# Expert results added to the tokens' rows in DRAM by accumulating indirect transfers, in a two-layer attention and mixture-of-experts kernel

## The chip, the cores and the metric

The kernel runs on one core of a Trainium2 chip. The metric is the device time of one execution in microseconds (us), as a median of several runs. TensorE (PE) multiplies matrices, VectorE (DVE) and ScalarE (ACT) work on tiles, GpSimd (POOL) works on tiles and issues the indirect transfers, and SyncE (SP) issues plain transfers, as ACT does too. An indirect transfer moves one row for each of 128 partitions, to or from the row of a DRAM table that a tile of indices names.

## The reference

Two layers over 2048 tokens of width 256. Each layer is cross-attention onto 154 context rows, then a mixture of 8 experts, of which each token uses two.

```python
x = x + L0_xattn(layernorm(x), ctx, ...)      # 16 heads
x = x + L0_ffn(layernorm(x), ...)             # 8 experts, top 2, inner width 1024, SiLU
x = x + L1_xattn(layernorm(x), ctx, ...)      # one head, with a bias that is given
x = x + L1_ffn(layernorm(x), ...)             # 8 experts, top 2, inner width 512, GELU
# L1_ffn: an expert keeps the first cap = 640 of its tokens, others are dropped
exp_batches = zeros((E, cap, d)).at[flat_e, pos_safe].set(x[tok], mode='drop')
exp_out = einsum('eci,eid->ecd', h, W2)
gathered = exp_out[flat_e, minimum(pos_safe, cap - 1)]
contrib = where(keep, gates_f, 0.0)[:, None] * gathered
out = segment_sum(contrib, tok, num_segments=N)
```

The last four lines are what the change touches: an expert's result for a token is scaled by the token's gate weight and added to the token's row, two results for each token.

## The kernel before

The sum `x` lies in SBUF as 16 tiles of 128 tokens, in 4 groups `g` of 4 tiles. All steps are written out by hand for each engine, in one program with semaphores; what stands behind a waiting instruction on its engine waits too.

A layer's mixture begins with routing. DVE's `choose`, `place` and `count` find each token's two experts, its slot in each (`slot_s`, expert times `REGION` plus position) and the two weights. POOL's `scatter(l, g)` (L520) sends each tile's normalised rows to the table `rows` in DRAM, once for each of the two choices: 8 indirect transfers for each group, 32 in a layer. SP's `clear_padding` fills the end of each expert's region with zeros. `count` writes a table of blocks: each expert has as many blocks of 256 rows as its tokens need, and PE does the last of them at half width where half is enough (21 blocks in layer 0 and 19 in layer 1 in this run).

`experts(l)` on PE, ACT and DVE then goes through the experts' blocks. In each block PE computes gate and up products in `pairs` steps (4 in layer 0, 2 in layer 1), ACT and DVE turn them into the hidden values in two float16 parts, PE turns the next block's rows (`turn_block`), and then multiplies down into PSUM banks 4 and 5. PE is up to two steps ahead of ACT and DVE, but the down product of block g waits for `y` of block g-1, since it writes the same banks. ACT ends a block by asking for the rows of block g+2 (`load`, L1087), copying the banks to the one buffer `yb` (L1111, signal `y`) and storing it in the table `results` (L1113).

Weights come beside that. SP fetches chunks of 512 KB into a ring of three, ACT makes the high part of each (`high_part`, L974) in the first block of the expert before, and POOL the low part (`low_parts`, L511: 6 chunks an expert in layer 0, 3 in layer 1). PE waits for the low parts of an expert before its first block.

When all blocks are stored, POOL gathers the results (`gather`, L544: two indirect transfers for each tile) and DVE adds them with their weights to `x` (`combine`, L1574 and L1576). Between the layers `combine_group(0)` and the layer norm behind it come ahead of PE's first work in layer 1 (`turn("a1", 0, ...)`, L620). In `layernorm` the tiny steps from L1193 to L1203 take an inverse square root. At the end, every combined tile is stored to the output.

## Time and profile before

| | us |
|---|---|
| median of 3 runs (1058.75 to 1060.64) | 1059.73 |
| the profiled execution, its own time | 1060.89 |
| its span | 1059.1 |

| engine | busy us | share of the span |
|---|---|---|
| PE | 749.0 | 71% |
| DVE | 540.3 | 51% |
| ACT | 392.6 | 37% |
| POOL | 374.8 | 35% |

The span is the profiled execution from its first to its last instruction; the run's own time is 1.8 us longer. Shares of busy time are means over stages with different limits, so each stage is read by itself. A row of the timeline gives the start, the duration, the engine, the line, the operation, what it writes and reads, and in brackets how long the engine was idle before it and what ended that. "issue" is time in which the engine waited for nothing that the profile shows.

### The profile page before, as it was taken

What the parts mean: (1) busy time and instruction counts of PE and PEld (TensorE: products, weight loads), DVE (VectorE), ACT (ScalarE), POOL (GpSimd) and SP (SyncE); (2) the same over time, 40 slices, a digit from 0 to 9 for tenths busy, and PEclk for the clock granted to TensorE, in tenths of its full rate; (3) what the DMA queues carried; (4) which work ended last, traced back from release to release, by engine and by line L of the source; (5) the groups of instructions that cost most, each with busy time, mean ns of one, the idle gap of its engine ahead of it and who ended that gap; (6) DMA issues with size and microseconds to landing.
All of it is one profiled execution on the core that took longest, in us unless ns stands there. A gap on an engine that the chain in (4) does not pass through costs nothing.

```text
span 1059.1 us, 18158 instructions
## 1 busy us (share of the span) xinstructions
PE 749.0 (71%) x6305; PEld 574.3 (54%) x6319; DVE 540.3 (51%) x1292; ACT 392.6 (37%) x668; POOL 374.8 (35%) x281
## 2 busy tenths in 40 slices
PE   5586969775249998998799891788734777777700
PEld 4243636534138887897588780354423665666600
DVE  7776768787514443453244643478652334434322
ACT  1136555593124354454445431222202344434300
POOL 7326005073724050451543407433232125132065
PEclk9888988797669999999899995666655999999955
DMA  4557114023324141541443213311013333241243
GB/s 122 149 117 272 31 34 117 1 85 123 110 70 159 40 139 40 159 139 42 139 156 99 89 39 90 100 40 41 35 43 129 120 119 127 91 148 50 69 129 119
DMA packets 68999, 103.81 MB, mean 98 GB/s; under 512 B 12406, under 2 KB 49923, under 8 KB 68956
## 3 DMA queue, kind: packets, MB, share of 16 engines
q1 hardware_dynamic: 39964, 64.82, 19.9%
q10 hardware_dynamic: 22848, 22.03, 6.5%
q0 software_dynamic: 6144, 16.44, 4.9%
q8 instruction: 21, 0.34, 0.1%
q14 instruction: 22, 0.18, 0.1%
HBM read 69.74 MB, written 33.87 MB: 98 GB/s over the span
## 4 chain that ended last, share of the span: by engine, by line
PE 39%; issue 25%; DVE 14%; ACT 9%; POOL 9%; DMA 3%; ACTq 1%; POOLq 0%; DVEq 0%
PE ps L595 36%; POOL probs L511 3%; DVE probs L1567 2%; POOL slot L511 2%; DVE probs L1495 2%; DVE mx L1350 2%; ACT probs L1034 2%; PE ps L620 1%; POOL rows L526 1%; DMA heads<-results,slot_g 1%; POOL heads L544 1%; ACT probs L1105 1%; ACT expo L1031 1%; DVE stats L1184 1%; ACT probs L974 1%
## 5 line engine op out<-in xcount | busy, mean ns | idle before, releaser
L1562 DVE TENSOR_TENSOR keys<-probs,ps 128x512 f32<-128x512 f32 x122 | 82.8, 687 | 304.3 <-PE ps L595 235.8
L595 PE MATMUL ps<-keys,probs 128*128 128x256 f16 (+1 forms) x1584 | 150.6, 257 | 25.3 <-issue 23.0
L595 PE MATMUL ps<-keys,slot 128*128 128x256 f16 (+1 forms) x1344 | 145.8, 273 | 20.8 <-issue 17.9
L511 POOL TENSOR_TENSOR probs<-inbox,probs 128x1024 f16<-128x1024 f32 x36 | 84.9, 2375 | 199.0 <-ACT probs L974 198.9
L595 PEld LDWEIGHTS ps<-keys,probs 128*128 128x128 f16 x1584 | 132.6, 99 | 41.9 <-issue 25.2
L595 PEld LDWEIGHTS ps<-keys,slot 128*128 128x128 f16 x1344 | 124.4, 102 | 41.0 <-issue 21.7
L511 POOL TENSOR_TENSOR slot<-inbox,slot 128x1024 f16<-128x1024 f32 x36 | 82.7, 2314 | 119.5 <-ACT slot L974 119.4
L1101 ACT ACTIVATE probs<-ps 128x512 f32<-128x512 f32 x122 | 71.4, 596 | 138.3 <-PE ps L595 135.1
L1567 DVE TENSOR_TENSOR probs<-keys,probs 128x512 f16<-128x512 f32 x122 | 116.6, 960 | 4.7 <-ACT probs L1105 1.9
L544 POOL DMA_INDIRECT heads<-results,slot_g x64 | 64.5, 1008 | 123.4 <-DMA results<-keys 79.2
L595 PE MATMUL ps<-probs 128*128 128x256 f16 x648 | 75.4, 273 | 16.0 <-DVE probs L1567 16.0
L1105 ACT CAST probs<-keys 128x512 f16<-128x512 f32 x122 | 74.8, 614 | 25.8 <-DVE keys L1562 25.6
L1495 DVE TENSOR_TENSOR probs<-expo,probs 128x512 f16<-128x512 f32 x80 | 63.7, 812 | 34.2 <-ACT probs L1034 33.9
L595 PE MATMUL ps<-slot,probs 128*128 128x256 f16 x600 | 69.7, 273 | 14.7 <-DVE probs L1567 14.7
L595 PEld LDWEIGHTS ps<-probs 128*128 128x128 f16 x648 | 61.1, 98 | 26.6 <-DVE probs L1567 19.5
L595 PEld LDWEIGHTS ps<-slot,probs 128*128 128x128 f16 x600 | 56.8, 98 | 24.4 <-DVE probs L1567 18.1
L1031 ACT ACTIVATE expo<-ps 128x512 f32<-128x512 f32 x80 | 47.8, 600 | 47.5 <-PE ps L595 44.6
L1111 ACT COPY keys<-ps 128x512 f32<-128x512 f32 x40 | 23.4, 585 | 111.1 <-PE ps L595 111.1
L526 POOL DMA_INDIRECT rows<-xp,slot_s x48 | 50.5, 1051 | 32.2 <-DVE slot_s L1434 16.6
L854 PE MATMUL ps<-identh,probs 128*128 128x128 f16 x336 | 26.4, 223 | 40.8 <-DMA probs<-rows 40.8
L1034 ACT CAST probs<-expo 128x512 f16<-128x512 f32 x80 | 49.0, 618 | 0.0
L555 POOL CAST xp<-xln 128x256 f16<-128x256 f32 x16 | 7.3, 456 | 113.0 <-ACT xln L981 111.5
(236 smaller groups left out, 1140.2 us busy)
## 6 DMA issues: line engine op xcount, KB each, us to landing
inbox<-in_W SPq DMA_DIRECT2D x24, 512.0 KB, 3.8
probs<-rows ACTq DMA_DIRECT2D x44, 256.0 KB, 2.7
results<-keys ACTq DMA_DIRECT2D x40, 256.0 KB, 2.1
inbox<-in_wg SPq DMA_DIRECT2D x16, 512.0 KB, 4.6
inbox<-in_wu SPq DMA_DIRECT2D x16, 512.0 KB, 3.5
inbox<-in_wd SPq DMA_DIRECT2D x16, 512.0 KB, 3.4
results<-zeros SPq DMA_DIRECT2D x6, 1024.0 KB, 10.9
rows<-zeros SPq DMA_DIRECT2D x16, 256.0 KB, 2.0
```

The lines of the kernel that those rows point to most:

```text
L511: pool.tensor_tensor(w_hl[slot][:, 1, at:at + CH], stage[:, n % STAGES, :], w_hl[slot][:, 0, at:at + CH], ALU.subtract).then_inc(S(f"w_rea ...
L526: pool.indirect_dma_start(out=rows, out_offset=bass.IndirectOffsetOnAxis(ap=slot_s[:, g * GT + t, k:k + 1], axis=0), in_=xps[g % 2 if l.n ...
L544: pool.indirect_dma_start(out=gb[:, t % GT, k, :], out_offset=None, in_=results, in_offset=bass.IndirectOffsetOnAxis(ap=slot_g[:, t, k:k + ...
L595: return pe.matmul(o, l, r, start=start, stop=stop, **kw)
L854: last = pe.transpose(psh[:, 6, part * BLK + hf * P:part * BLK + (hf + 1) * P], x_raw[:, hf, part * P:(part + 1) * P], identh[:, :])
L1031: act.activation(e_ring[:, u % 4, :], ps[:, 4 + u % 2, :], ACT.Exp, scale=float(DK) ** -0.5).then_inc(S("a0_exp"), 1)
L1034: act.copy(p_hi[:, u - 1, :], e_ring[:, (u - 1) % 4, :]).then_inc(S("a0_phi"), 1)
L1101: act.activation(s_act[:, j % 2, :], ps[:, 2 * (j % 2), :], l.act).then_inc(S(r + "_s"), 1)
L1105: act.copy(h_hi[:, 2 * j - 2:2 * j, :].rearrange("p c t -> p (c t)"), h32[:, (j - 1) % 2, :]).then_inc(S(r + "_hh"), 1)
L1495: dve.tensor_tensor(p_lo[:, u, :], e_ring[:, u % 4, :], p_hi[:, u, :], ALU.subtract).then_inc(S("a0_plo"), 1)
L1562: dve.tensor_tensor(h32[:, j % 2, :], s_act[:, j % 2, :], ps[:, 2 * (j % 2) + 1, :], ALU.mult).then_inc(S(r + "_h32"), 1)
L1567: dve.tensor_tensor(h_lo[:, 2 * j - 2:2 * j, :].rearrange("p c t -> p (c t)"), h32[:, (j - 1) % 2, :], h_hi[:, 2 * j - 2:2 * j, :].rearran ...
```

## The change

ACT no longer copies a block's result out of PSUM; it scales each row by its weight on the way (two activations with a scale for each partition) and stores nothing. Weight and token number of each slot come from a new DRAM table `meta` (8 bytes a row), loaded for each block into the tile `carried`. POOL fills that table by 32 more indirect transfers in each layer (`scatter_weights`), and for each block it issues two indirect transfers that add `yb`'s rows to the tokens' rows in a DRAM array (`add_results`): `attended` in layer 0, the output itself in layer 1. Both start as a copy of `x`, which SP writes (`keep_rows`). Between the layers SP loads `attended` back into `x`. The table `results`, its filling with zeros, the gathers, the adding on DVE and the stores at the end are gone, and so are the index and weight steps of DVE that served them. A row past the end of an expert's tokens has the token number `FAR`, which is out of bounds, and so is skipped.

```diff
+            def keep_rows(l, g, signal):
+                sp.dma_start(l.sums[g * GW:(g + 1) * GW, :].rearrange("(t p) d -> p t d", p=P), x[:, g * GT:(g + 1) * GT, :]).then_inc(S(signal), 16)
+            def added(l):
+                total = sp.value_load(table[l.n][0:1, 8:9], min_val=1, max_val=MAXBLK)
+                wait_counted(sp, S(l.r + "_added"), total + 1)
...
-            for n in range(k0 + STAGES):
+            for n in range(STAGES):
+                fetch(L[0], 0, n)
+            for g in range(NG - 1):
+                sp.wait_ge(S("a0_x"), 2 * (g + 1))
+                keep_rows(L[0], g, "r0_kept")
+            for n in range(STAGES, k0 + STAGES):
                 fetch(L[0], n // k0, n % k0)
...
+                if e == 0:
+                    added(L[0])
+                    for g in range(NG):
+                        sp.dma_start(x[:, g * GT:(g + 1) * GT, :],
+                                     attended[g * GW:(g + 1) * GW, :].rearrange("(t p) d -> p t d", p=P)).then_inc(S(f"r0_x{g}"), 16)
...
+            def add_results(l, e):
+                tb, r = table[l.n], l.r
+                first = pool.value_load(tb[0:1, bass.ds(e, 1)], min_val=0, max_val=MAXBLK - 1)
+                end = pool.value_load(tb[0:1, bass.ds(e + 1, 1)], min_val=1, max_val=MAXBLK)
+                with pool.Fori(first, end) as g:
+                    wait_counted(pool, S(r + "_y"), g + 2)
+                    for hf in range(2):
+                        pool.indirect_dma_start(
+                            out=l.sums, out_offset=bass.IndirectOffsetOnAxis(ap=carried[:, hf, 1:2].bitcast(I32), axis=0),
+                            in_=yb[:, hf, :], in_offset=None, bounds_check=N - 1, oob_is_err=False,
+                            compute_op=ALU.add).then_inc(S(r + "_stored"), 16)
+                    pool.wait_ge(S(r + "_stored"), g * 32 + 32)
+                    pool.sem_inc(S(r + "_added"), 1)
...
             def rest_of_experts(l):
+                pool.wait_ge(S(l.r + "_kept"), 16 * NG)
+                pool.wait_ge(S(l.r + "_table"), 1)
                 low_parts(l, 1, 1, range(len(l.chunks)))
-                with pool.Fori(1, E // 2) as pr:
+                add_results(l, 0)
+                with pool.Fori(0, E // 2 - 1) as pr:
                     for slot in range(2):
-                        low_parts(l, pr * 2 + slot, slot, range(len(l.chunks)))
+                        low_parts(l, pr * 2 + slot + 2, slot, range(len(l.chunks)))
+                        add_results(l, pr * 2 + slot + 1)
+                add_results(l, E - 1)
...
+            def scatter_weights(l, g):
+                for t in range(GT):
                     for k in range(TOP):
                         pool.indirect_dma_start(
-                            out=gb[:, t % GT, k, :], out_offset=None, in_=results,
...
+                            out=l.meta, out_offset=bass.IndirectOffsetOnAxis(ap=slot_s[:, g * GT + t, k:k + 1], axis=0),
+                            in_=sent[:, g * GT + t, k, :], in_offset=None, bounds_check=E * REGION - 1,
+                            oob_is_err=False).then_inc(S(f"{r}_meta"), 16)
...
+                def load_carried(g):
+                    row = act.value_load(tb[0:1, bass.ds(g + TB_ROW, 1)], min_val=0, max_val=E * REGION - BLK)
+                    act.wait_ge(S(r + "_added"), g + 1)
+                    act.dma_start(carried[:, :, :], l.meta[bass.ds(row, BLK), :].rearrange("(h p) d -> p h d", p=P)).then_inc(S(r + "_carried"), 16)
...
                     load(g + 2)
+                    load_carried(g)
                     act.wait_ge(S(r + "_down"), g + 2)
-                    act.wait_ge(S(r + "_stored"), g * 16 + 16)
-                    act.copy(yb[:, :, :], ps[:, 4:6, 0:D]).then_inc(S(r + "_y"), 1)
-                    act.wait_ge(S(r + "_y"), g + 2)
-                    act.dma_start(results[bass.ds(g * BLK, BLK), :].rearrange("(h p) d -> p h d", p=P), yb[:, :, :]).then_inc(S(r + "_stored"), 16)
+                    act.wait_ge(S(r + "_carried"), g * 16 + 16)
+                    for hf in range(2):
+                        ins = act.activation(yb[:, hf, :], ps[:, 4 + hf, 0:D], ACT.Identity, scale=carried[:, hf, 0:1])
+                    ins.then_inc(S(r + "_y"), 1)
...
                 load(1)
+                act.wait_ge(S(r + "_meta"), 16 * NT * TOP)
                 with act.Fori(0, E // 2 - 1) as pr:
...
-            def combine(l, t):
+            def rows_summed(g):
+                dve.wait_ge(S(f"r0_x{g}"), 16)
                 layernorm("a1", g, xln, g)
```

On POOL, the order changes at three kinds of places. First the end of routing in layer 0, where `rows` is the table of the tokens' rows. Before:

```order
L557 TENSOR_TENSOR xp<-xln,xp 128x256 [waits pool_step]
L526 DMA rows<-xp,slot_s 18432x512 [waits r0_slot,r0_xp]
L526 DMA rows<-xp,slot_s 18432x512 x7
L511 TENSOR_TENSOR probs<-inbox,probs 128x1024 [waits w_hi0] x6
L516 UNCONDITIONAL_BRANCH
```

And of the changed kernel, where the lines are other numbers for the same code and `meta` is the new table:

```order
L573 DMA rows<-xp,slot_s 18432x512 [waits r0_slot,r0_xp]
L573 DMA rows<-xp,slot_s 18432x512 x7
L585 DMA meta<-sent,slot_s 18432x2 x16
L538 TENSOR_TENSOR probs<-inbox,probs 128x1024 [waits w_hi0,r0_table,r0_kept]
L538 TENSOR_TENSOR probs<-inbox,probs 128x1024 [waits w_hi0] x5
```

Sixteen transfers of groups 2 and 3 now stand behind the last rows; those of groups 0 and 1 stand behind their own groups' rows. Layer 1 has the same order. Next on POOL, the end of layer 0's experts. Before:

```order
L516 REGISTER_ALU
L516 COMPARE_AND_BRANCH
L573 TENSOR_TENSOR betas<-betas 128x1 [waits ld_phi]
L575 TENSOR_TENSOR betas<-betas 128x1 [waits pool_step]
L577 TENSOR_SCALAR keys<-keys,betas 128x2464 [waits pool_step]
L533 TENSOR_LOAD table
```

And of the changed kernel, with the last expert's loop of adding ahead:

```order
L549 DMA attended<-keys,carried 2048x256 [waits r0_y]
L549 DMA attended<-keys,carried 2048x256
L553 ISA
L546 REGISTER_ALU [waits r0_stored]
L546 COMPARE_AND_BRANCH
L618 TENSOR_TENSOR betas<-betas 128x1 [waits ld_phi]
L620 TENSOR_TENSOR betas<-betas 128x1 [waits pool_step]
L622 TENSOR_SCALAR keys<-keys,betas 128x2464 [waits pool_step]
L538 TENSOR_TENSOR slot<-inbox,slot 128x1024 [waits w_hi1] x3
```

The scaling of the attention bias (`keys` here, `phi` in the source) was free to run once the last low parts were made; now it and layer 1's first low parts stand behind the last block's adding. Last on ACT, the end of a block in layer 0. Before:

```order
L1087 DMA probs<-rows 128x2x512
L1109 REGISTER_ALU
L1110 ISA [waits r0_down]
L1111 COPY keys<-ps 128x512 [waits r0_stored]
L1113 ISA [waits r0_y]
L1113 DMA results<-keys 128x2x256
```

And of the changed kernel:

```order
L1128 DMA probs<-rows 128x2x512
L1132 ISA
L1132 TENSOR_LOAD table
L1132 ISA x2
L1133 REGISTER_ALU
L1134 ISA [waits r0_added]
L1134 DMA carried<-meta 128x2x2
L1157 REGISTER_ALU
L1158 ISA [waits r0_down]
L1160 ACTIVATE keys<-ps,carried 128x256 [waits r0_carried]
```

Here the wait for the adding of the block before stands ahead of the load of `carried`, and that load ahead of the result's way out of PSUM (`keys` holds `yb`). The store is gone.

## Rows read from the trace of the kernel before

**Rows 1.** Stages: length; busy us of PE, PEld, DVE, ACT, POOL; clock, DMA share, GB/s.
```profile
1006.00:1059.00 53.00, 0.00 (x0) 0.00 (x0) 15.51 (x32) 0.00 (x0) 32.15 (x32) 0.51 0.41 124
```

**Rows 2.** Timeline, the end: start, us, instruction, idle before and releaser.
```profile
1004.89 0.58 ACT L1111 COPY keys<-ps 128x512 f32<-128x512 f32 x1 [1.86 <-PE ps L595]
...
1008.70 1.06 POOL L544 DMA_INDIRECT heads<-results,slot_g  x1 [34.53 <-DMA results<-keys]
...
1052.68 0.48 DVE L1576 SCALAR_TENSOR_TENSOR x<-heads,weight,x 128x256 f32<-128x256 f32 x1
```

**Rows 3.** Timeline between the layers.
```profile
634.93 0.59 ACT L1111 COPY keys<-ps 128x512 f32<-128x512 f32 x1 [1.72 <-PE ps L595]
...
651.93 1.41 DVE L1184 BATCH_NORM_STATS2 stats<-x 128x6 f32<-128x256 f32 x4
...
654.25 0.16 DVE L1199 TENSOR_TENSOR rt<-ry_a 128x4 f32<-128x4 f32 x1
...
657.64 1.97 PE L620 MATMUL ps<-ident,xln 128*128 128x128 f32 x8 [22.82 <-issue]
...
659.48 6.28 POOL L511 TENSOR_TENSOR slot<-inbox,slot 128x1024 f16<-128x1024 f32 x3
```

**Rows 4.** Timeline, the start of layer 0's experts.
```profile
295.32 0.97 POOL L526 DMA_INDIRECT rows<-xp,slot_s  x1 [0.30 <-issue]
...
305.29 1.28 ACT L1101 ACT_TABLE_LOAD   x1 [31.69 <-issue]
307.50 12.12 PE L595 MATMUL ps<-keys,slot 128*128 128x256 f16 x96 [4.89 <-issue]
310.27 0.60 ACT L1101 ACTIVATE probs<-ps 128x512 f32<-128x512 f32 x1 [3.70 <-PE ps L595]
```

**Rows 5.** The chain of waits: start, us from an indirect transfer's start to its landing.
```profile
295.32 2.42 DMA rows<-xp,slot_s
...
800.89 2.65 DMA rows<-penalties,slot_s
...
1010.06 2.84 DMA heads<-results,slot_g
```

**Rows 6.** Timeline, the start of layer 1's experts.
```profile
814.09 0.60 ACT L1101 ACTIVATE probs<-ps 128x512 f32<-128x512 f32 x1
...
819.46 1.48 PE L595 MATMUL ps<-slot,probs 128*128 128x256 f16 x12 [0.94 <-DVE probs L1567]
```

**Rows 7.** Timeline, two places where POOL and DVE work on SBUF together.
```profile
241.50 6.28 POOL L511 TENSOR_TENSOR slot<-inbox,slot 128x1024 f16<-128x1024 f32 x3
241.53 7.42 DVE L1495 TENSOR_TENSOR probs<-expo,probs 128x512 f16<-128x512 f32 x2 [0.96 <-ACT probs L1034]
...
587.56 6.52 POOL L577 TENSOR_SCALAR keys<-keys,betas 128x2464 f32<-128x2464 f32 x1
...
588.43 5.47 DVE L1567 TENSOR_TENSOR probs<-keys,probs 128x512 f16<-128x512 f32 x1
...
593.96 4.19 PE L595 MATMUL ps<-slot,probs 128*128 128x256 f16 x36 [1.79 <-DVE probs L1567]
```

**Rows 8.** Timeline, POOL and ACT in layer 1's first experts.
```profile
818.93 7.08 POOL L511 TENSOR_TENSOR probs<-inbox,probs 128x1024 f16<-128x1024 f32 x3 [17.06 <-ACT probs L974]
...
830.35 0.38 ACTq L1087 DMA_DIRECT2D probs<-rows  x1
...
833.06 0.59 ACT L1111 COPY keys<-ps 128x512 f32<-128x512 f32 x1 [2.91 <-PE ps L595]
...
839.22 0.58 ACT L1111 COPY keys<-ps 128x512 f32<-128x512 f32 x1 [1.85 <-PE ps L595]
...
867.51 0.58 ACT L1111 COPY keys<-ps 128x512 f32<-128x512 f32 x1 [1.85 <-PE ps L595]
```

**Rows 9.** DMA issues: queue, count, KB each, median us from issue to landing.
```profile
probs<-rows ACTq DMA_DIRECT2D x44, 256.0 KB, 2.7
...
k_rest<-k_out SPq DMA_DIRECT2D x24, 3.2 KB, 1.8
```

More of the change, by code:

```diff
@@ L88, in two_layers @@
         k_out = nc.dram_tensor("k_out", (B, 2, D, SK), F16, kind="Internal").ap()
-        results = nc.dram_tensor("results", (MAXBLK * BLK, D), F32, kind="Internal").ap()
+        meta = [nc.dram_tensor(f"meta{n}", (E * REGION, 2), F32, kind="Internal").ap() for n in range(2)]
+        attended = nc.dram_tensor("attended", (N, D), F32, kind="Internal").ap()
         WS = 6144
@@ L243, in two_layers @@
         oh = sb("oh", [P, NT, TOP, E])
-        pos_kept = sb("pos_kept", [P, NT, TOP])
-        weight = sb("weight", [P, NT, TOP])
+        sent = sb("sent", [P, NT, TOP, 2])
+        weight, token = sent[:, :, :, 0], sent[:, :, :, 1].bitcast(I32)
+        nowhere = sb("nowhere", [P, 16, 2])
+        carried = sb("carried", [P, 2, 2])
         slot_s = sb("slot_s", [P, NT, TOP], I32)
-        slot_g = sb("slot_g", [P, NT, TOP], I32)
         cnt = sb("cnt", [P, E])
@@ L265, in two_layers @@
         yb, keys_at = part(keys, keys_at, [P, 2, D])
-        gb, _ = part(heads, 0, [P, GT, TOP, D])
         class Layer:
@@ L279, in two_layers @@
             l.pairs = l.hc // 2
+            l.meta, l.sums = meta[n], (attended, out)[n]
             l.cap = (N, N * TOP * 5 // 4 // E)[n]
@@ L434, in _ @@
                     fetch(L[1], e, n)
+                if e == 0:
[3 more added lines that the diff above has]
+                                     attended[g * GW:(g + 1) * GW, :].rearrange("(t p) d -> p t d", p=P)).then_inc(S(f"r0_x{g}"), 16)
+            for g in range(NG):
+                sp.wait_ge(S("a1_x"), GT * (g + 1))
+                keep_rows(L[1], g, "r1_kept")
             clear_padding(L[1])
@@ L438, in _ @@
                     fetch(L[1], e, n)
-            for t in range(NT):
-                sp.wait_ge(S("r1_x"), t + 1)
-                sp.dma_start(out[t * P:(t + 1) * P, :], x[:, t, :]).then_inc(S("stored"), 16)
-            sp.wait_ge(S("stored"), 16 * NT)
+            sp.wait_ge(S("r1_kept"), 16 * NG)
+            added(L[1])
         @block.gpsimd
@@ L1597, in _ @@
                 if g + 1 < NG:
-                    combine_group(g + 1)
+                    rows_summed(g + 1)
                 if g:
@@ L1621, in _ @@
             experts(L[1])
-            for t in range(NT):
-                combine(L[1], t)
 def kernel(**inputs):
```

87 lines of the change are left out of this document (33 added, 54 removed).

## The prediction, written before the result was known

> **What bounds the kernel now.** I read first the stages, then the chain of waits, then the timeline where the chain changes engine. In the last 53 us PE does nothing at all [rows 1]. The last result leaves PSUM at 1004.89 and POOL starts to gather at 1008.70; the last of DVE's additions starts at 1052.68 [rows 2]. The reader sees a queue of 32 indirect transfers there, one each 1.27 us: 0.97 busy and 0.30 idle [rows 4]. The same happens between the layers, but there only one group of four tiles stands ahead of PE: the last copy starts at 634.93 and PE's first work at 657.64 [rows 3]. In the experts themselves PE sets the pace, and POOL is mostly idle.
>
> The sum is made against the profiled execution's own time, 1060.89; the median is 1.2 us less, and I carry the difference over to it.
>
> **The unknown price.** No row shows an accumulating transfer. Call L the time from its start to its landing. It is the write of the same 1 KB rows, which takes 2.42 to 2.65, with a read of the destination ahead, and the gather as a whole takes 2.84 [rows 5]. So L lies between 2.65 (the read is hidden) and 5.5 (a read and then a write, 2.84 + 2.65). Of the nearest row, 2.65, some 0.85 is left beyond the 1.8 that a load of 3.2 KB takes [rows 9]; doubling this part gives 3.5, which I take.
>
> [...]
>
> **The change part by part.**
>
> *Start of layer 0's experts, +10.* Sixteen transfers of weights stand behind the last rows. The last row transfer starts at 295.32, so the sixteenth starts at 295.32 + 16 x 1.27 = 315.7 and lands 2.65 later, at 318.3 [rows 4, 5]. ACT must have them before its first block. A wake-up with a read of the table took 0.95 on POOL (the landing at 1007.75, which is 1005.64 + 2.11, to 1008.70) [rows 2]; with the table load of 1.28 the first activation comes at 320.6, where it now starts at 310.27 [rows 4]. PE can do two of its four steps of 3.0 meanwhile (12.12 for four). Its third step now starts at 313.5; after, it waits for the activation and DVE's product, 0.6 each: 321.8, so +8.3. The waits for groups 0 and 1 lie in POOL's idle time. But the eight transfers of group 1 push three low parts from 241.50 to about 252. DVE's last two subtractions there take 7.42 now, since they stand still until POOL's 6.28 are over [rows 7]; freed, DVE and PE gain about 5, and then the head outputs meet the same low parts ten us later, until 258. SP's wait for the third group's rows also delays a weight chunk. Between -4 and +4, I take +1.7.
>
> *Layer 0's experts, -1.* Scaling in two pieces costs at most 0.6 more than one copy (0.58), and the store's issue goes. A full block lasts three to four times L, so its adding is hidden; if that cover went, each short block would pay what L exceeds. The bias scaling of 6.52 leaves the middle of the experts, where it stopped DVE for 5.47 and PE for 1.79 [rows 7]: -1.8. What is left of the late scalings I put at +0.8.
>
> *Between the layers, +1.* ACT asks for a block's weights about 1 after the next rows, they land 2.1 later and are scaled in 1.0, so the result is ready 4.1 after the rows' load; the copy of a full block ends 3.3 after it now (830.35 to 833.65 [rows 8]), and a short block has less room. I take 2 late, 637.5 instead of 635.5. POOL starts 0.9 later, and the landing is at 638.4 + 3.5 = 641.9 (in a short block the second transfer has no rows). Sixteen gathers, 1.27 each, are off POOL. But phi (6.52) and three low parts (6.28, [rows 3]) now begin only there: 641.9 to 654.7. The loads of `attended` are 512 KB; half of that in rows of 1 KB lands in 2.7 [rows 9], so 2.7 to 5.4, and I take 4: 645.9. DVE's statistics can run, but from the first tiny product of two SBUF tiles (654.25, 3.4 before PE's 657.64 [rows 3]) it would wait for POOL to end. PE starts at 654.7 + 3.4 = 658.1, with the betas' small steps 658.5: +1.
>
> The rows on which this rests are DVE's 5.47 for one subtraction beside POOL's scaling of phi, to whose end it lasts (593.9 and 594.1), and the 7.42 beside three low parts in a row [rows 7]. The Trainium skill says the same as a rule (SBUF — State Buffer, "Who interferes with whom"): a VectorE instruction with two SBUF inputs blocks fully against a GpSimd instruction that reads SBUF. Without it the part would come to -6, which is the second case below.
>
> *Attention of layer 1, 0.* DVE's adding and POOL's gathers go, but they stand beside PE's products. The copies of `x` (4 of 512 KB) are hidden there too; a late one would show before the low parts of expert 1.
>
> *Start of layer 1's experts, +10.* As in layer 0: 800.89 + 16 x 1.27 = 821.2, landing 823.9, wake-up 0.95, table load 1.28: first activation at 826.1 against 814.09. PE's down product comes 5.4 after it at 819.46, because PE is then still in its first steps [rows 6]; after, both steps are done, and two activations, product, cast and subtraction of 0.6 to 0.7 each leave 3.3. So 829.4: +9.9.
>
> *Layer 1's experts, +11.* Here the added wait decides. From result to result runs one chain: POOL's wake-up 0.9, one issue 1.3, L 3.5, the load of `carried` 2.1 (1.8 for 3.2 KB, at most 2.7 [rows 9]) and two scalings 1.0: 8.8. A short block now follows a full one in 6.2 (833.06 to 839.22 [rows 8]), so it comes 2.6 late. The full block before is late too: POOL makes low parts first, 818.93 to 826.0, and adds then, so `carried` is asked for at 826.0 + 1 + 4.8 = 831.8 and not at 831.4 (the load of rows at 830.35 and 1 us): +1.4 with the scaling. Queued behind the waiting load on ACT are the result, which PE's next down product waits for, and the next expert's first activation. That comes about 3.5 late, of which PE's two steps ahead hide half: +1.7. Five experts of three blocks are followed by another, 5 x 1.7 = 8.5, and the last short block adds 2.6. As a check, POOL's cycle in such an expert is 7.1 + 1 + 4.8 + 4 + 4.8 + 4 + 3.5 = 29.2, against 28.3 now (839.22 to 867.51 [rows 8]): POOL is just about to be the bound. Each us of L beyond this enters about 16 times.
>
> *The end, -45.5.* From 1005.5 to the span's end are 53.6 now. After: wake-up 0.9, landing 3.7 from the start, and the closing. That is between 0 and 5.9 (1053.16 to 1059.1 now, with a store in it); without the store's 2.1 about 3.5. So 8.1.
>
> Sum: 10 - 1 + 1 + 10 + 11 - 45.5 = -14.5, that is 1046.4 for the profiled execution and 1045 for the median. 6 MB of zeros less at the start I count at nothing: PE and DVE work through them.
>
> **The rivals.**
>
> *A slow addition: POOL's chain becomes the bound of layer 1's experts.* Price 16 x (L - 3.5). It decides from L = 3.5 + 14.5/16 = 4.4; at 5.5 the experts take 32 more, and with a few us at the short blocks of layer 0 the time is 1080. For it: a transfer that reads, adds and writes each of 128 rows has no row here, and POOL waits for it with nothing overlapped. Against it: the gather's own read of DRAM adds only 0.2 to the write's 2.65 [rows 5].
>
> *A fast addition and a free port.* L = 2.65 takes about 5 from layer 1's experts, 1 from the end and 1 between the layers, and DVE getting through between POOL's instructions takes 7 there: 1031. Against it stands the 7.42 of [rows 7].
>
> *The gain goes to POOL's new queue at the starts.* If the transfers of 8-byte pieces drain more slowly than POOL issues them, each start pays more; at 2 us each instead of 1.27 that is 12 per layer, and the time 1069. The Trainium skill, DMA: Bandwidth & Descriptors, "Specifications", says that writes under 512 B are done as read-modify-write. No row shows its price, so this case has a small chance.
>
> **How the numbers follow.** Forecast as worked out, L from 3 to 4: 0.52, 1036 to 1056. Fast addition: 0.14. Slow addition from 4.4 up: 0.24. Between the two, about no change: 0.05. Slow small pieces: 0.05. This kernel's measurement tells 0.2% (2 us) from no change. Faster: 0.52 + 0.14 and 0.02 of the case between = 0.68; the same: 0.03 of it and 0.03 at the edges = 0.06; slower: the rest, 0.26. The range from 1033 to 1076 leaves out one in ten on either side; the likeliest case's own range is 1036 to 1056.
>
> **What would show it.** The landing of the adding transfers, 3.5 from the start. The first activation of layer 0's experts near 320, of layer 1's 12 later than now relative to its routing. DVE's tiny products between the layers standing still until the low parts of layer 1 end. Short blocks in layer 1 8.8 after their full ones, and ACT idle before its scaling, released by POOL's adding. The span's end 8 after the last result. The prediction is wrong if L is over 4.4 or if the end keeps more than 15 of its 53.6.

## The result, and the profile after

Before: 1060.04 us median of 20 runs. After: 1063.03 us median of 20 runs. The ratio is 1.0036, 95% interval 1.0023 to 1.0048: slower by 3 us, or 0.36%, where 0.2% is taken as no change. The forecast was 1045, with 0.26 for slower. The profiled execution of the changed kernel took 1063.5 us (span 1061.7) against 1060.9 (span 1059.1) before.

The two spans cut at the same events (last transfer of `rows` issued, first and last result leaving PSUM, PE's first work of layer 1; all read from the timelines):

| stage | before | after | difference | forecast |
|---|---|---|---|---|
| start to the last rows of layer 0 | 295.3 | 298.0 | +2.7 | with the next |
| to the first result of layer 0 | 30.1 | 41.8 | +11.8 | +10 |
| layer 0's results, first to last | 309.5 | 309.8 | +0.3 | -1 |
| to PE's first work of layer 1 | 22.7 | 22.8 | +0.1 | +1 |
| to the last rows of layer 1 | 143.3 | 141.4 | -1.9 | 0 |
| to the first result of layer 1 | 22.7 | 33.2 | +10.5 | +10 |
| layer 1's results, first to last | 181.3 | 201.1 | +19.8 | +11 |
| to the end | 54.2 | 13.5 | -40.7 | -45.5 |

The four large steps (the two starts, layer 1's experts and the end) went the way they were worked out. Three of them cost more or gained less than forecast, layer 1's experts most, and the fourth, the start of layer 1's experts, was met. Single stages that no edit touches differ by 2 us and more between traces: layer 0's experts, in their form of before, take 309.5 here and 311.5 and 311.6 in two later runs.

The end first. The row of stages (columns as in [rows 1]) shows the 12 us that stand where [rows 1] has 53, and the timeline under it answers to [rows 2]:

```profile
1049.00:1061.00 12.00, 0.00 (x0) 0.00 (x0) 0.00 (x0) 0.00 (x0) 3.10 (x2) 0.50 0.07 7
```

```profile
1048.12 0.84 ACT L1160 ACTIVATE keys<-ps,carried 128x256 f32<-128x256 f32 x2 [6.36 <-DMA carried<-meta]
1049.84 1.55 POOL L549 DMA_INDIRECT out_x<-keys,carried  x1 [6.58 <-ACT keys L1160]
1051.69 1.55 POOL L549 DMA_INDIRECT out_x<-keys,carried  x1 [0.30 <-issue]
```

The gathers and the adding on DVE are gone. But one issue of an adding transfer takes 1.55, not the 0.97 of [rows 4], and after the last landing, 1054.4 in the trace's raw record, comes a closing wait of POOL's that the timeline doesn't print: its drain, 6.77 us, to 1061.4. That is 7.0 after the landing. The raw record of the kernel before has the same: the landing that releases DVE's last adding is at 1051.93 and POOL's drain ends at 1058.88, 6.95 later.

The line of the adding transfers, with their durations (ns, min/median/max) and the time from start to landing:

```profile
L549 POOL DMA_INDIRECT out_x<-keys,carried x38: 1547/1550/1824, 849.4 to 1051.7; - x38
...
DMA to landing us min/median/max: 2.7/3.8/7.6
```

The costliest groups (columns: busy us, mean ns of one | idle before, releaser) show where ACT waits now: 135.6 of 179.4 us of idle time ahead of the scaling are ended by the load of `carried`:

```profile
L1160 ACT ACTIVATE keys<-ps,carried 128x256 f32<-128x256 f32 x80 | 33.6, 471 | 179.4 <-DMA carried<-meta 135.6
```

Layer 1's experts, as the chain of waits goes through them (start, us, what), for one block, from a result to the next; this answers to [rows 8]:

```profile
857.48 0.48 ACT keys L1160
...
858.83 0.34 POOL out_x L549
859.17 1.52 issue
860.69 3.96 DMA out_x<-keys,carried
...
864.85 1.96 DMA carried<-meta
...
867.24 0.43 ACT keys L1160
```

Two scalings take 0.84, POOL's wake-up 0.88, its first transfer until the second may start 1.86, the landing of the second 3.96, ACT's wake-up 0.2 and the load of `carried` 1.98: 9.72 from 857.11 to 866.83. PE is on none of it. The stages of both kernels (first row before, second after) show that PE waits and that its granted clock falls with that, 0.97 to 0.90, so that the same products also take 8.6 us more:

```profile
824.00:1006.00 182.00, 136.23 (x1364) 116.09 (x1362) 68.90 (x90) 71.84 (x111) 44.49 (x19) 0.97 0.31 102
```

```profile
847.00:1049.00 202.00, 144.82 (x1368) 120.22 (x1365) 66.92 (x90) 76.28 (x130) 98.69 (x56) 0.90 0.39 87
```

The start of layer 0's experts, the timeline that answers to [rows 4]:

```profile
298.04 0.98 POOL L573 DMA_INDIRECT rows<-xp,slot_s  x1 [0.30 <-issue]
...
305.90 1.01 PE L895 MATMUL ps<-identh,probs 128*128 128x128 f16 x8 [27.39 <-DMA probs<-rows]
...
313.07 7.18 PE L636 MATMUL ps<-keys,slot 128*128 128x256 f16 x48 [6.16 <-issue]
323.06 1.28 ACT L1148 ACT_TABLE_LOAD   x1 [46.74 <-issue]
324.35 1.08 ACT L1148 ACTIVATE probs<-ps 128x512 f32<-128x512 f32 x2
...
325.89 7.59 PE L636 MATMUL ps<-keys,slot 128*128 128x256 f16 x48 [5.64 <-DVE keys L1602]
...
333.76 5.40 PE L636 MATMUL ps<-slot,probs 128*128 128x256 f16 x48
...
339.88 0.84 ACT L1160 ACTIVATE keys<-ps,carried 128x256 f32<-128x256 f32 x2 [4.02 <-DMA carried<-meta]
```

The chain of waits shows when the last small transfer has landed:

```profile
318.50 3.06 DMA meta<-sent,slot_s
```

The chain runs from this landing through ACT's wake-up and table load to the first activation, and from there through PE. PE itself starts 15.0 after the last rows, 12.2 before, a thing the forecast didn't have; but that costs nothing here, since PE has done its two steps at 320.3 and waits 5.64 until DVE has taken the first. The wait of 4.02 for `carried` costs at most 0.7: PE's down product ends at 339.16.

Between the layers, which answers to [rows 3]:

```profile
656.12 2.03 SPq L456 DMA_DIRECT2D x<-attended  x4
...
656.84 6.52 POOL L622 TENSOR_SCALAR keys<-keys,betas 128x2464 f32<-128x2464 f32 x1
659.98 1.41 DVE L1231 BATCH_NORM_STATS2 stats<-x 128x6 f32<-128x256 f32 x4 [12.32 <-DMA x<-attended]
...
661.84 1.54 DVE L1240 TENSOR_SCALAR ve<-mv_a 128x4 f32<-128x4 f32 x1
663.34 6.27 POOL L538 TENSOR_TENSOR slot<-inbox,slot 128x1024 f16<-128x1024 f32 x3
663.41 2.07 DVE L1243 TENSOR_SCALAR ry_a<-ve 128x4 int32<-128x4 int32 x1
...
669.67 0.16 DVE L1250 SCALAR_TENSOR_TENSOR ry_a<-rt,ry_a 128x4 f32<-128x4 f32 x1
...
672.49 1.97 PE L661 MATMUL ps<-ident,xln 128*128 128x128 f32 x8 [24.54 <-DVE xln L1270]
```

The statistics run beside POOL's scaling at full speed (1.41 for four, as in [rows 3]); each tiny step after them takes until POOL's instruction in progress ends, four of them 1.5 to 2.1 instead of 0.17. The first two are scalings with one input in SBUF, not the tiny products that the forecast took to be the first to stop. The Trainium skill, SBUF — State Buffer, "Who interferes with whom", has `tensor_scalar` among the operations that can take the port pair shared with GpSimd; these rows agree.

### The profile page after: what moved, and what is told of

It reads as the page before. It is cut to its first block, busy times and chain, and to the rows that moved or that the text cites. A ratio compares the mean times of both kernels' runs of the same rounds, so it can differ in the third digit from the quotient of the medians.

```text
span 1061.7 us, 18824 instructions
## 1 busy us (share of the span) xinstructions
PE 761.7 (72%) x6305; PEld 580.0 (55%) x6319; DVE 507.1 (48%) x1186; ACT 400.1 (38%) x708; POOL 493.9 (47%) x365
## 4 chain that ended last, share of the span: by engine, by line
PE 34%; issue 15%; DVE 14%; DMA 14%; POOL 10%; ACT 10%; ACTq 2%; POOLq 1%; DVEq 0%; SPq 0%
PE ps L636 31%; DMA out_x<-keys,carried 5%; DMA carried<-meta 4%; POOL probs L538 4%; POOL meta L585 3%; DVE probs L1535 2%; DMA attended<-keys,carried 2%; DVE mx L1397 2%; PE ps L661 2%; ACT probs L1075 2%; ACT slot L1015 1%; DVE keys L1602 1%; POOL out_x L549 1%; DMA inbox<-in_wu 1%; ACT expo L1072 1%
## 5 line engine op out<-in xcount | busy, mean ns | idle before, releaser
L636 PE MATMUL ps<-keys,probs 128*128 128x256 f16 (+1 forms) x1584 | 154.7, 261 | 26.9 <-issue 23.2
L636 PE MATMUL ps<-keys,slot 128*128 128x256 f16 (+1 forms) x1344 | 142.7, 269 | 27.4 <-issue 18.0
L549 POOL DMA_INDIRECT attended<-keys,carried x42 | 68.5, 1630 | 117.6 <-ACT keys L1160 110.1
L538 POOL TENSOR_TENSOR probs<-inbox,probs 128x1024 f16<-128x1024 f32 x36 | 82.1, 2299 | 41.3 <-ACT probs L1015 37.7
L1160 ACT ACTIVATE keys<-ps,carried 128x256 f32<-128x256 f32 x80 | 33.6, 471 | 179.4 <-DMA carried<-meta 135.6
L549 POOL DMA_INDIRECT out_x<-keys,carried x38 | 59.4, 1562 | 84.7 <-ACT keys L1160 70.6
L636 PE MATMUL ps<-slot,probs 128*128 128x256 f16 x600 | 74.6, 285 | 25.1 <-DVE probs L1607 25.1
L636 PEld LDWEIGHTS ps<-probs 128*128 128x128 f16 x648 | 61.4, 99 | 33.4 <-DVE probs L1607 25.5
L636 PEld LDWEIGHTS ps<-slot,probs 128*128 128x128 f16 x600 | 59.3, 102 | 36.9 <-DVE probs L1607 28.3
L1535 DVE TENSOR_TENSOR probs<-expo,probs 128x512 f16<-128x512 f32 x80 | 58.5, 742 | 39.7 <-ACT probs L1075 39.5
L585 POOL DMA_INDIRECT meta<-sent,slot_s x64 | 63.3, 989 | 19.5 <-issue 19.5
L895 PE MATMUL ps<-identh,probs 128*128 128x128 f16 x336 | 26.4, 223 | 45.5 <-DMA probs<-rows 45.5
```

The costliest lines, as they stand in the source:

```text
L538: pool.tensor_tensor(w_hl[slot][:, 1, at:at + CH], stage[:, n % STAGES, :], w_hl[slot][:, 0, at:at + CH], ALU.subtract).then_inc(S(f"w_rea ...
L549: pool.indirect_dma_start(out=l.sums, out_offset=bass.IndirectOffsetOnAxis(ap=carried[:, hf, 1:2].bitcast(I32), axis=0), in_=yb[:, hf, :], ...
L585: pool.indirect_dma_start(out=l.meta, out_offset=bass.IndirectOffsetOnAxis(ap=slot_s[:, g * GT + t, k:k + 1], axis=0), in_=sent[:, g * GT ...
L636: return pe.matmul(o, l, r, start=start, stop=stop, **kw)
L1160: ins = act.activation(yb[:, hf, :], ps[:, 4 + hf, 0:D], ACT.Identity, scale=carried[:, hf, 0:1])
L1535: dve.tensor_tensor(p_lo[:, u, :], e_ring[:, u % 4, :], p_hi[:, u, :], ALU.subtract).then_inc(S("a0_plo"), 1)
```

## The experiments

There are four sets of runs, and in each the kernel before was timed beside the others on the same chip: `late_meta`, `l1_plain`, `carried_early` and `phi_early` first (the median of the kernel before is 1059.5), `meta_hold`, `two_buffers` and `all_three` second (1061.8), the runs named `_pinned` and `renumbered` third (1060.3), `l1_only`, `l1_two` and `all_three_again` last (1059.5). The first two sets ran on one chip, the third and the last on two others. Ratios are to the kernel before of the same set, with 95% intervals.

**The wait for the weights.** `late_meta`:

```diff
                 load(1)
-                act.wait_ge(S(r + "_meta"), 16 * NT * TOP)
...
                     act.wait_ge(S(r + "_added"), g + 1)
+                    act.wait_ge(S(r + "_meta"), 16 * NT * TOP)
                     act.dma_start(carried[:, :, :], ...
```

> The same kernel, but ACT waits for the transfers of weights only before its first load of `carried`, not before its first activation. Theory A (the 16 transfers of 8-byte pieces cost only because ACT stands still behind them): first activation of layer 0's experts back to about 311 from 324.3, first result at 328 from 339.9 (last transfer lands at 321.1, the load of `carried` takes 2, PE's down product is the later one); in layer 1 the last piece lands at 336.4 after the start of layer 1's own clock (836.4 in the profile of the change), so the first result comes about 7.5 earlier than 847.1. In sum -19, 1044. Rival B (POOL stands still behind these transfers anyway, and the low parts of the next expert or the shared port pass the delay on): at most -5, 1058.

Measured: 1053.99, ratio 0.9955 (0.9929 to 0.9980). Half of what A said. The first result of layer 0 comes at 333.0, 339.9 in the change and 325.4 before; from layer 1's last rows to its first result it takes 27.8, 33.2 in the change and 22.7 before. So in both layers ACT's wait is about half of what the start costs. The timeline of the start shows what remains:

```profile
298.03 0.45 ACTq L1128 DMA_DIRECT2D probs<-rows  x1
303.20 1.01 PE L895 MATMUL ps<-identh,probs 128*128 128x128 f16 x8 [28.70 <-DMA probs<-rows]
...
310.70 9.47 PE L636 MATMUL ps<-keys,slot 128*128 128x256 f16 x64 [6.49 <-issue]
...
328.01 0.38 ACTq L1135 DMA_DIRECT2D carried<-meta  x1
...
332.98 0.84 ACT L1161 ACTIVATE keys<-ps,carried 128x256 f32<-128x256 f32 x2 [6.05 <-DMA carried<-meta]
```

The load of rows takes 5.2 to PE's first turning (298.77 to 301.59 before, 2.8), and the small load of `carried` 5.0, while SP fetches weights. Here both are on the chain of waits. `meta_hold` tests the first: `late_meta`, and ahead of the last 16 transfers of each layer

```diff
+            pool.wait_ge(S("r0_xraw"), 32)
             scatter_weights(L[0], 2)
             scatter_weights(L[0], 3)
```

> As the kernel with the late wait, but POOL starts the last 16 transfers of weights of a layer only when both loads of rows have landed. Theory C (the 8-byte transfers slow the loads of rows that run beside them: 5.2 instead of 2.8 from issue to landing): the first load lands in 2.8 again and PE starts layer 0's experts 12.4 after the last transfer of rows, not 16.1; the weights come about 5 later, so that the first result of layer 0 comes 36 to 37 after the last rows (38.4 with the late wait alone), that of layer 1 about 5 later than there; in all 1057. Rival D (the zeros that SP writes, or something else, slow those loads): 5 again, PE 16 after the last rows, and 1060.

Measured 1112.04, ratio 1.0458 (1.0427 to 1.0488), with the last rows of layer 0 at 309.7, ahead of anything that the edit touches. The cause is taken up below. The same kernel with its semaphores in the order of the change, `meta_hold_pinned` (a list of all names is allocated first):

> meta_hold with the semaphores' numbers of the change. Theory E: no standstills; with theory C (the 8-byte transfers slow the loads of rows) PE starts layer 0's experts 12.4 after the last transfer of rows, and the time is 1057 against 1054 of the late wait alone; with theory D PE starts 16 after it. Rival F: 1112 again.

Measured 1072.41, ratio 1.0119 (1.0099 to 1.0139). Its start:

```profile
299.29 4.93 ACTq L1154 DMA_DIRECT2D probs<-rows  x2
302.04 1.01 PE L921 MATMUL ps<-identh,probs 128*128 128x128 f16 x8 [25.66 <-DMA probs<-rows]
...
307.89 12.19 PE L662 MATMUL ps<-keys,slot 128*128 128x256 f16 x96 [4.84 <-issue]
...
328.65 6.29 POOL L562 TENSOR_TENSOR probs<-inbox,probs 128x1024 f16<-128x1024 f32 x3
330.82 0.34 SPq L435 DMA_DIRECT2D inbox<-in_wu  x1
...
336.34 1.04 ACT L1041 CAST probs<-inbox 128x1024 f16<-128x1024 f32 x1 [14.89 <-DMA inbox<-in_wu]
```

Theory C holds: without the small transfers beside it the load lands in 2.75, and PE starts 12.0 after the last rows. The total went the other way, and the rows say why: the low parts of expert 1 stand behind the transfers on POOL, SP can't refill the ring of chunks until they are made, and ACT stands 14.89 for a chunk, ahead of the block's result (44.8 after the last rows). In layer 1 the first result comes 39.3 after the last rows, 11.5 later than in `late_meta`, the larger part of the loss. POOL's queue reaches PE by three ways: the weights of the tokens, the loads beside it, and the low parts.

**The chain of one buffer.** `l1_plain`:

```diff
-                            compute_op=ALU.add).then_inc(S(r + "_stored"), 16)
+                            **({} if l.n else dict(compute_op=ALU.add))).then_inc(S(r + "_stored"), 16)
```

> In layer 1 alone the transfers of results overwrite the token's row instead of adding to it, so the output lacks the sum. Theory A (adding is what makes one issue 1.55 instead of 0.97 and the landing 3.96 instead of 2.65): the chain of layer 1's blocks shortens by 2 x 0.58 + 1.3 = 2.5 to 7.2, its experts take 186 instead of 201 from first to last result, the end 2 less: about 1046. Rival B (the size and the place of the rows make the price, not the adding): issue, landing and time unchanged within 2.

Measured 1051.38, ratio 0.9920 (0.9891 to 0.9949); layer 1's results span 184.9, short blocks follow in 7.5. Both kinds of transfer stand in this one trace, by their line (ns) and by the list of issues (last number: median us to landing):

```profile
L549 POOL DMA_INDIRECT attended<-keys,carried x42: 1547/1555/1889, 346.1 to 656.3; - x42
L549 POOL DMA_INDIRECT out_x<-keys,carried x38: 972/974/998, 854.1 to 1040.1; - x38
```

```profile
attended<-keys,carried POOLq DMA_INDIRECT x42, 3.8
out_x<-keys,carried POOLq DMA_INDIRECT x38, 2.4
```

Adding costs 0.58 an issue and 1.4 a landing, and 16 us in layer 1 (theory A; B has fallen). The end did not get shorter (14.0): POOL's drain takes 8.4 here, and why is open.

`carried_early`: a second tile, loaded behind the result of the block before.

```diff
-                    load_carried(g)
                     act.wait_ge(S(r + "_down"), g + 2)
                     act.wait_ge(S(r + "_carried"), g * 16 + 16)
+                    act.wait_ge(S(r + "_added"), g + 1)
...
+                    act.copy(carried[:, :, 1:2].bitcast(I32), coming_w[:, :, 1:2].bitcast(I32)).then_inc(S(r + "_y"), 1)
+                    act.wait_ge(S(r + "_y"), g + 2)
+                    load_carried(g + 1)
```

> The weights and token numbers of a block are loaded a block ahead into a second small tile; when the adding of the block before has landed, ACT scales from it and copies the token numbers over. Theory A (in layer 1 one chain through ACT, POOL, the adding transfer and the load of `carried` sets the pace, 9.7 from result to result): the chain loses the load, about 1.8, and comes to 8.0; full blocks fall back to 9.5, short ones to 8.0; layer 1's experts take 190 from first to last result instead of 201, the short blocks of layer 0 come 0.9 earlier each, the last block before the attention 1.8: in sum about -13, 1050. Rival B (POOL with its low parts and the adding is itself the bound in layer 1): at most -3, 1060.

Measured 1067.79, ratio 1.0083 (1.0056 to 1.0111): slower, where A said 1050. In layer 1 A holds (192.8 from first to last result, full blocks 9.4, short ones 7.6 to 8.5), but layer 0 takes 321.3. ACT reads the table and issues the load (at 420.41) between the result and the next activation, where PE waits for it:

```profile
418.43 0.84 ACT L1160 ACTIVATE keys<-ps,coming_w 128x256 f32<-128x256 f32 x2 [4.50 <-PE ps L637]
419.16 0.19 ACT L1161 COPY carried<-coming_w 128x2 int32<-128x2 int32 x1
...
421.32 1.09 ACT L1148 ACTIVATE probs<-ps 128x512 f32<-128x512 f32 x2 [1.97 <-PE ps L637]
```

The activation starts 2.9 after the scaling; in the change it is 0.7 (415.93, 416.66). Full blocks of layer 0 take 16.9, not 15.4 to 16.2.

`two_buffers`: `yb` has two sides (in the tile `heads`), `carried` four places; the load of block g+1 stands in ACT's idle time ahead of the wait for the down product. So it takes two things off the chain, the one buffer and the load.

```diff
-                    load_carried(g)
+                    act.wait_ge(S(r + "_carried"), g * 16 + 16)
+                    load_carried(g + 1)
                     act.wait_ge(S(r + "_down"), g + 2)
+                    wait_counted(act, S(r + "_added"), g + 1)      # that semaphore starts one higher: block g-2
+                    for side in range(2):
+                        with act.If(g % 2 if side else 1 - g % 2):
...
+                    pool.tensor_copy(to_rows[:, :], carried[:, bass.ds((g % 4) * 2, 2), 1:2]...)
```

> The starts are as in the change. `yb` has two sides, `carried` four places, loaded a block ahead ahead of the wait for the down product; ACT scales block g as soon as the adding of block g-2 has landed, POOL copies the token numbers to a small tile and adds in the same order as in the change. Theory A (one buffer for the results makes ACT, POOL, the adding and the load one chain): layer 1's experts go from 200 to 187 from first to last result, where POOL's own round (7.5 a block, and 6.3 of low parts an expert) is the next bound; layer 0's short blocks come 0.9 earlier; -14 in all, 1049. Rival B (the chain is POOL's alone, and ACT waits for it whatever the buffers): layer 1's experts 197 or more, 1060.

> The kernel with two buffers and the semaphores' numbers of the change. Theories A and E: layer 1's experts 183.5 as in the run with the other numbers, the front and the attention of layer 1 as in the change, 1063 - 17 = 1046. Rival F: 1090 again.

The first took 1090.72, ratio 1.0285 (1.0250 to 1.0320), the pinned one 1051.35, ratio 0.9908 (0.9880 to 0.9936). Layer 1's results span 183.5 and 184.8 (201.1 in the change). Its first short block waits for PE, not for a load:

```profile
857.50 0.84 ACT L1190 ACTIVATE heads<-ps,carried 128x256 f32<-128x256 f32 x2 [3.54 <-DMA carried<-meta]
...
863.63 0.84 ACT L1190 ACTIVATE heads<-ps,carried 128x256 f32<-128x256 f32 x2 [2.67 <-PE ps L664]
866.96 0.18 POOL L572 COPY to_rows<-carried 128x2 int32 x1 [3.36 <-DMA out_x<-heads,to_rows]
```

Short blocks follow in 6.1 to 6.5, as before the change (6.2). Theory A holds: the loss of layer 1's experts is this chain. Of the 16.3 that it gives back there, `carried_early`, which took the load alone off the chain, had 8.2; what the second side of `yb` would give without the earlier load was not run. POOL lags behind with its adding, so that the next low parts come late and PE stands 8.6 after the third expert's single block, which costs 4.

**The port between the layers.** `phi_early`: POOL's scaling of the bias one call earlier.

```diff
+                if l.n == 0:
+                    scale_phi()
                 add_results(l, E - 1)
```

> POOL scales the attention bias before the last expert's adding of layer 0, not behind it. Theory A (between the layers DVE's tiny steps stand still until POOL's instruction in progress ends: 1.5 to 2.1 each instead of 0.17): from the last result of layer 0 to PE's first work in layer 1 16.5 instead of 22.8, and up to 2 lost in the experts: -4, 1059. Rival B (the load of `attended` is what PE waits for): no change between the layers, the total the same or 2 more.

Measured 1057.49, ratio 0.9984 (0.9965 to 1.0003), 5.5 less than the change's median. From the last result to PE's first work it takes 16.3 instead of 22.8, as A has it. Part of that is paid ahead of it: the scaling now runs at 632.64 beside a full block of the last expert, where from result to result 18.8 pass (16.5 in the change), and layer 0's experts take 315.7 in all (309.8 in the change, at most 312.9 in four others). The rows between the layers:

```profile
660.86 6.28 POOL L538 TENSOR_TENSOR slot<-inbox,slot 128x1024 f16<-128x1024 f32 x3 [1.48 <-DMA attended<-keys,carried]
664.50 1.40 DVE L1234 BATCH_NORM_STATS2 stats<-x 128x6 f32<-128x256 f32 x4 [12.36 <-DMA x<-attended]
666.35 0.81 DVE L1243 TENSOR_SCALAR ve<-mv_a 128x4 f32<-128x4 f32 x1
667.20 0.17 DVE L1246 TENSOR_SCALAR ry_a<-ve 128x4 int32<-128x4 int32 x1
```

**Together, and 40 us that stay unexplained.** `all_three` joins `two_buffers`, the late wait and `phi_early`; `renumbered` is the change with meta_hold's semaphore numbers and no other edit.

> Two buffers, the wait for the weights only before their first load, and the attention bias scaled before the last adding of layer 0, together. If the three losses are separate (theory A), their gains add: 14 + 9 + 5.5, and the time is 1034. If one mends what another has mended (theory B: after an earlier start the same chain or the same port is waited for), 1045 or more.

> All three mendings with the semaphores' numbers of the change. Theories A and E with separate gains: 17 + 9 + 5.5 off 1063, 1032. If one mends what another has mended: 1045. Rival F: 1087 again.

> The change itself, instruction for instruction, with its semaphores in the order in which the kernel meta_hold happened to allocate them: from the 68th on each has a number one or two higher. In meta_hold and in the two kernels with two buffers ACT and DVE stand still for 5 to 21 at a time on PE's signals (194.5, 262.2, 785.1 and 830.1 in meta_hold), at places that their edits don't touch, and all three number their semaphores otherwise than the change. Theory E (the numbers cost the time): 1063 becomes about 1110, with the same standstills. Rival F (the edits cost it, by way of the program's code or POOL's order): 1063 as before.

`all_three` took 1086.84, ratio 1.0228 (1.0205 to 1.0251); pinned 1042.32, ratio 0.9822 (0.9803 to 0.9842); `renumbered` 1066.80, ratio 1.0073 (1.0054 to 1.0093). In `meta_hold`, `two_buffers` and `all_three` DVE and ACT stand for signals of PE whose products the trace puts long before ("remote" means that it has no instruction that released them); of `meta_hold`, where PE's last product before this row ends at 815.1:

```profile
830.14 1.66 DVE L1642 SCALAR_TENSOR_TENSOR x<-ps,rd,x 128x256 f32<-128x256 f32 x4 [21.12 <-remote]
```

The semaphores' numbers alone (E) gave 4, not 47, so E had fallen, and yet the pinned kernels lost nothing. The decider was the same file again, `all_three_again`:

> The kernel with all three mendings, with the semaphores' numbers that it had at first (1087 then, 1042 with the numbers of the change). Theory E2 (the numbers cost the time, but only together with the edits, since the change alone in other numbers took 1067): 1087 again, with the standstills of ACT and DVE at the same places. Rival G (something of the chip or the hour in that set of three runs): 1042.

Measured 1040.92, ratio 0.9822 (0.9805 to 0.9838), without one such standstill. The same file ran 46 apart, so its edits and numbers alone don't cost the 40; something of the second set did (rival G), though the kernel before ran at 1061.8 in it. The chip and the hour are not told apart: the second set's chip had run the first set without standstills, and all repeats were made on others. `meta_hold` and `two_buffers` were not repeated in their first numbers. What it was stays open, and the totals of that set are not used.

The three mendings overlap. By themselves they took 11.7 (`two_buffers_pinned`), 9.0 and 5.5 off the change, 26.2 in all; together it is 20.7, between A and B. In the traces the scaling's earlier place costs 6.0 in layer 0's experts (315.0 against 309.0 in `two_buffers_pinned`), and the late wait saves 2.8 at layer 1's start instead of 5.4.

**One layer alone.** `l1_only` is the kernel before with the change in layer 1 only; `l1_two` is that with two buffers and the late wait.

```diff
 def rest_of_experts(l):                      # l1_only, on the kernel before
...
+                if l.n:
+                    add_results(l, 0)
...
+                        ins = act.activation(yb[:, hf, :], ps[:, 4 + hf, 0:D], ACT.Identity, scale=carried[:, hf, 0:1])
...
-            for t in range(NT):
-                combine(L[1], t)
```

> The kernel before, with the change in layer 1 alone (layer 0 keeps its table of results, the gathers and the adding on DVE). From the stages of the two profiles: front, layer 0 and the way between the layers as before (first result of layer 0 30 after the last rows, 309.5 for its experts, 22.7 between), layer 1's start +10.5, its experts 199 to 201 instead of 181, the end 13.6 instead of 54.2: 1060 + 10.5 + 19 - 40.6 = 1049, minus 2 in the attention where POOL has no gathers beside it. If the change's parts lean on each other (rival), it differs from this sum by more than 4.

> The same with two sides of `yb` and four places of `carried` and the late wait for the weights. Theory A: layer 1's experts 185 instead of 200, its start +5 to +8 instead of +10.5, all else as in l1_only: 1049 - 15 - 4 = 1030, and so faster than the kernel with all three mendings in both layers (1042), since layer 0 gains nothing from the change. Rival: layer 0 in its new form was not a loss, and this one is no faster than 1042.

`l1_only`: 1051.07, ratio 0.9913 (0.9892 to 0.9934). Its stages: 295.4, 30.9, 311.6, 22.8, 142.1, 33.4, 201.1, 13.7, in the order of the table. They are those of the kernel before in layer 0 and those of the change in layer 1, each within 2.1, but the total is 4 above the expected sum (1047), just at the bound beyond which the parts were to count as leaning on each other. So they add up to about 4. `l1_two`: 1035.88, ratio 0.9774 (0.9758 to 0.9790), the fastest of all: 24 us below the kernel before and 27 below the change. It missed its 1030. Layer 1's start stays 33.2: its chain goes through all sixteen small transfers (the last lands at 827.4) and then through a load of `carried` of 5.0. And the end takes 17.0, since POOL is still at the block before when the last result is ready:

```profile
1019.52 0.84 ACT L1205 ACTIVATE heads<-ps,carried 128x256 f32<-128x256 f32 x2 [2.84 <-issue]
1023.18 0.18 POOL L560 COPY to_rows<-carried 128x2 int32 x1 [3.03 <-DMA out_x<-heads,to_rows]
```

## Why the prediction was wrong

The forecast for the profiled execution was 1046.4; it took 1063.5. Layer 1's experts are half of the 17 us, the end and layer 0's start most of the rest. With layer 1's experts as forecast the kernel would have gained about 6 instead of losing 3, still far from the 14.5 of the forecast. Neither of the prediction's own signs of being wrong came: L is 3.8 to 3.96, below 4.4, and the end keeps 12.7 of its 53.6. By its steps:

- *Layer 1's experts, +11*: +19.8. This is the step that failed. The mechanism was right (the added wait, one chain from result to result, `carried` on it), and the landing was nearly right (3.8 in the median, 3.96 in the chain; 3.5 taken). What was wrong is "one issue 1.3": the price of a plain transfer was given to an adding one, which takes 1.55 + 0.30 = 1.86, as `l1_plain` shows in one trace. The issue is 0.56 of what was missing and the landing 0.46; the other terms take 0.1 back. With both the chain is 9.7, not 8.8, and so longer than PE's full block of 9.4 too, which the sum had left out. The two runs at 7.5 (184.9) and 9.7 (201.1) put one us of the chain at 7.2, as an estimate; by that the forecast's own 8.8 would have given 194.5, or +13.2, and the missed 0.9 the other 6.6. So the forecast's +11 was too low even for its own chain, and its 16 per us was too steep.
- *The end, -45.5*: -40.7. The landing stood at 3.7 from the start and takes 4.6 (the second transfer starts 1.85 after the first and lands in 2.73). The closing stood at 3.5, chosen between 0 and 5.9, and takes 7.2 from the landing to the span's end. The prediction counted it from DVE's last adding and took the store as part of it. But before, too, the end was set by POOL's drain, which ran beside the last adding and the store: it ends at 1058.9, 7.0 after the last gather's landing, when SP has long been done (1055.0).
- *Start of layer 0's experts, +10*: +11.8, and 2.7 more were there before the last rows (298.0; nine other traces with the change in both layers, outside the second set, have 293.7 to 297.7, the kernel before 295.3). The queue was right to 0.1 (the last transfer starts 20.46 after the last rows, 20.32 in the forecast). The missing 1.8 are its landing (3.06, not 2.65), ACT's wake-up (1.5, not 0.95) and up to 0.7 of waiting for `carried` at the first result. The slower load of rows, 4.4 instead of 2.8, was missed too, but lies beside ACT's wait and costs only once that is mended: `late_meta` shows that ACT's wait was half of what the start costs (6.9 of 14.5, counted from the span's start). The rival of slow 8-byte pieces had the wrong mechanism: POOL issues them at 1.28 as any other; it is their neighbours that are slowed.
- *Between the layers, +1*: +0.1; the port lock is shown by `phi_early`. In the rows of the change one DVE step gets through at each end of a POOL instruction, and the steps are quick only when POOL has stopped at 669.6; the forecast let none through, which comes to the same.
- *Layer 0's experts, -1* and *attention, 0*: +0.3 and -1.9. Four other traces with these blocks as in the change have 310.7 to 312.9 in place of 309.8, and three with them as before 309.5 to 311.6, so no effect of the change on these blocks is shown either way.
- *Start of layer 1's experts, +10*: +10.5. Right in size; but with the late wait 27.8 of 33.2 remain, where 22.7 is what it was.

Of the rivals, the slow addition had its turning point at L = 4.4, 0.9 more on the chain, and the kernel landed at that chain and near that time. That is partly luck: by its price of 16 per us this 0.9 would have used up the whole gain, but it made 6.6, and the rest came from the other steps. Bounding L from both sides while fixing the issue, which no row showed either, made the range of the chain too narrow.

## What to carry to other kernels

An indirect transfer that adds is a new instruction on its queue: give its issue a bound of its own, and look for a loop in which issue, landing and the next load follow each other on one buffer; a second buffer together with an earlier load was worth 16 us here, the adding itself 16 in one layer, and both measure the same chain. At the end of a program, look for what ends last in the raw record and count from the event that starts it: here 7 us stand behind the last landing, before and after the change. Where two layers share a change, price each: here layer 0 had nothing at its end to gain and paid 12 (1063.0 against 1051.1 in `l1_only`), and layer 1 alone with two buffers is 2.3% faster than before.

## What the runs showed of the hardware

- The issue of an adding indirect transfer of 128 rows of 1 KB keeps POOL busy for 1.55 us, a plain one for 0.97; landing 3.8 against 2.4 from the start. The Trainium skill (Collectives: The Full Stack, "The bandwidth ceiling: the fold count and why AG ≠ RS ≠ AR") says that a reduce step of a collective reads two sources and so runs at about half the rate of a copy step. It says so of large transfers in a ring of four ranks; here adding makes the landing 1.6 times and the issue 1.6 times as long, so its factor of two isn't met.
- Loads of 256 KB beside indirect transfers of 8-byte rows land in 4.4 to 5.2 us (the change and `late_meta`), in 2.75 when these are held back (`meta_hold_pinned`).
- POOL's closing drain ends 7.0 us after the landing of the last indirect transfer, in the change (adding ones) as in the kernel before (gathers), 7.3 after it in `l1_only` and `l1_two`, and 8.6 in `l1_plain`. So adding isn't what sets it; what does is not shown.
- Within one set of runs three kernels lost about 40 us while another ran as ever; only a repeat of the same file, in another set and on another chip, told this from an effect of the edits.
